# Seventeen groups of work in place of sixteen, the first and the last with one batch each

## The reference

```
x = x + layernorm(attn(layernorm(x)))
x = x + layernorm(ffn(layernorm(x)))

attn(x): x = x + lif(time_mix(layer_norm(x, ln1_s, ln1_b)))
         x = x + lif(channel_mix(layer_norm(x, ln2_s, ln2_b)))
  time_mix:    k, v, r = mixes of x and x shifted by one step, times Wk, Wv, Wr
               sigmoid(r) * wkv(w_decay, u_first, k, v) @ Wo     (a scan over time)
  channel_mix: sigmoid(xr @ Wr) * (square(relu(xk @ fWk)) @ fWv)     (128 -> 512 -> 128)
  lif:         a leaky integrate-and-fire scan over time that gives spikes 0 or 1
ffn(x):  h = silu(x @ w1) * (x @ w2)      (128 -> 512, ternary weights, a scale per output)
         h = gelu(h @ h1);  h = gelu(h @ h2)      (512 -> 512, twice)
         h @ w3                                   (512 -> 128)
```

## Time and profile before

| | |
|---|---|
| median of 3 runs | 652.96 us (652.8 to 653.86) |
| the profiled execution | 655.56 us, of which 653.6 us span from first to last instruction |
| PE busy | 585.9 us (90%), 2241 matmuls |
| DVE busy | 556.2 us (85%) |
| ACT busy | 535.6 us (82%) |
| POOL busy | 418.9 us (64%) |
| mean granted TensorE clock | 0.97 |
| HBM | 12.14 MB read, 4.19 MB written |

### The profile page before, as it was taken

The page is one execution under the profiler, slowest core; times in us unless marked ns, Lnnn a source line. Parts: engine busy times, 40 slices in busy tenths (PEclk is TensorE's granted clock), DMA queues, the critical chain, the costliest instruction groups (busy, mean ns, idle before and its releaser), DMA issues. The chain is left out here.

```text
span 653.6 us, 9756 instructions
## 1 busy us (share of the span) xinstructions
PE 585.9 (90%) x2241; PEld 361.9 (55%) x2241; DVE 556.2 (85%) x1538; ACT 535.6 (82%) x849; POOL 418.9 (64%) x571
## 2 busy tenths in 40 slices
PE   1366699999999999999999999999999999999994
PEld 0122256575656666565756565665756566656662
DVE  2978899989899999999999999999899899875543
ACT  4776587979798998979797988979797988967773
POOL 4553447677767768767677677686757675553442
PEclk9778799999999999999999999999999999999998
DMA  8010000000010101010000101010000101000001
GB/s 292 2 33 17 19 17 17 16 19 16 18 33 18 33 18 33 18 34 1 21 29 18 32 19 32 18 33 18 18 17 1 34 2 33 2 16 2 16 2 32
DMA packets 26574, 17.02 MB, mean 26 GB/s; under 512 B 1168, under 2 KB 25744, under 8 KB 26256
## 3 DMA queue, kind: packets, MB, share of 16 engines
q1 hardware_dynamic: 26512, 16.34, 8.1%
HBM read 12.14 MB, written 4.19 MB: 25 GB/s over the span
## 5 line engine op out<-in xcount | busy, mean ns | idle before, releaser
L906 ACT ACTIVATE hid<-p_f,scale 128x512 f32<-128x512 f32 x128 | 87.9, 687 | 65.0 <-PE p_f L2255 64.6
L2255 PE MATMUL p_f<-a_lo,w_hi 128*128 128x512 f32 x320 | 134.2, 419 | 1.6 <-DVE a_lo L289 0.7
L2255 PE MATMUL p_f<-a_hi,w_hi 128*128 128x512 f32 x320 | 125.9, 394 | 0.0
L2255 PE MATMUL p_f<-b_lo,w_hi 128*128 128x512 f32 x256 | 111.4, 435 | 2.3 <-DVE b_lo L289 0.9
L2255 PE MATMUL p_f<-b_hi,w_hi 128*128 128x512 f32 x256 | 100.6, 393 | 0.0
L900 ACT ACTIVATE a_hi<-hid 128x512 fp32r<-128x512 f32 x128 | 79.1, 627 | 2.9 <-DVE hid L1640 1.6
L432 POOL TENSOR_TENSOR nd<-factors,pq 128x512 f32<-128x512 f32 x32 | 38.7, 1210 | 63.3 <-DVE pq L1507 63.3
L289 DVE TENSOR_TENSOR a_lo<-hid,a_hi 128x512 fp32r<-128x512 f32 x96 | 65.6, 703 | 9.5 <-ACT a_hi L900 8.9
L2255 PEld LDWEIGHTS p_f<-a_lo,w_hi 128*128 128x128 f32 x320 | 60.3, 188 | 21.1 <-issue 7.0
L416 POOL TENSOR_TENSOR rstd<-var,minus_half 128x4 f32<-128x4 f32 x64 | 70.0, 1098 | 2.2
L289 POOL TENSOR_TENSOR b_lo<-hid,b_hi 128x512 fp32r<-128x512 f32 x32 | 45.4, 1430 | 38.7 <-DVE fired_all L1548 26.3
(11 more groups left out here) (143 smaller groups left out, 1437.5 us busy)
## 6 DMA issues: line engine op xcount, KB each, us to landing
xa<-in_x SPq DMA_DIRECT2D x16, 256.0 KB, 2.8
xb<-in_x SPq DMA_DIRECT2D x16, 256.0 KB, 3.1
out<-y_out SPq DMA_DIRECT2D x15, 256.0 KB, 3.5
kk<-in_ffn SPq DMA_DIRECT2D x1, 1024.0 KB, 7.0
hid<-in_ffn SPq DMA_DIRECT2D x1, 1024.0 KB, 9.6
mix<-in_mix SPq DMA_DIRECT2D x1, 512.0 KB, 6.2
gate<-in_ffn SPq DMA_DIRECT2D x1, 512.0 KB, 5.6
mix<-in_mix SPq DMA_DIRECT2D x1, 320.0 KB, 3.8
```

The lines of the kernel that those rows point to most:

```text
L906: act.activation(hid[:, m], p_f[m % 2][:, :], ACT.Gelu, scale=scale[:, 1 + layer, m:m + 1]).then_inc(s_gelu[layer], 1)
L2255: last = pe.matmul(out_, w[:, b], x[:, k], start=(k == 0 and t == 0), stop=(k == n - 1 and t == len(terms) - 1))
```

## The change

There are 17 groups. Group 0 and group 16 hold one batch (256 columns, two token tiles); groups 1 to 15 hold two. Every instruction of a one-batch group is cut to `0:g.w` columns, `0:g.nb` batches or `0:g.j` tiles; its number of instructions stays, except that what is issued per tile or per batch is issued half as often. The written orders of all engines are laid anew, in `opening`, `onset`, `turn` and `ending`; turn still runs for i = 5 to 12, and the ending has one more group. In the last group the two blocks of each hidden layer that are computed first are taken in parts (three input blocks each, then the fourth). Its last product takes the fourth input block as one fp32 product from `hid` itself, so its `high(3, 3)` and `low(3, 3)` are gone. Its statistics are taken from `p_turn` directly, and the copy to tokens runs after them.

Cut to its core:

```diff
-GROUPS_IN_ALL = 16
+GROUPS_IN_ALL = 17
+ROWS = 256
+TILES = 2
...
         self.par = n % 2
         self.turn = n // 2
+        self.nb = 1 if n in (0, GROUPS_IN_ALL - 1) else 2
+        self.first = max(2 * n - 1, 0)
+        self.w = self.nb * ROWS
+        self.j = self.nb * TILES
...
-    GROUPS = B // NB
+    GROUPS = B // NB + 1
...
-    x_tiles = x_in.rearrange("(g b) (h p) c -> g p (b h) c", b=NB, p=P)
-    out_tiles = out.rearrange("(g b) (h p) c -> g p (b h) c", b=NB, p=P)
+    def tiles(t, g):
+        return t[g.first:g.first + g.nb].rearrange("b (h p) c -> p (b h) c", p=P)
...
-                sp.dma_start(xa[:, g.par], x_tiles[g.n]).then_inc(s_xa[g.par], 16)
+                sp.dma_start(xa[:, g.par, 0:g.j], tiles(x_in, g)).then_inc(s_xa[g.par], 16)
...
-                sp.dma_start(out_tiles[GROUPS - 1][:, 2 * h:2 * h + 2],
-                             y_out[:, 2 * h:2 * h + 2]).then_inc(s_stored, 16)
+                sp.dma_start(tiles(out, G[GROUPS - 1])[:, h:h + 1], y_out[:, h:h + 1]).then_inc(s_stored, 16)
             sp.wait_ge(s_stored, 16 * (GROUPS + 1))
...
-                act.activation(hid[:, m], p_f[m % 2][:, :], ACT.Gelu,
+                act.activation(hid[:, m, 0:g.w], p_f[m % 2][:, 0:g.w], ACT.Gelu,
                                scale=scale[:, 1 + layer, m:m + 1]).then_inc(s_gelu[layer], 1)
...
+            def last_tokens(g):
+                act.wait_ge(s_bn[5], g.n + 1)
+                wait(act, s_y_out, g.n)
+                act.activation(f_out[:, 0:g.j], p_turn[:, 0:g.w].rearrange("p (j c) -> p j c", c=C),
+                               ACT.Copy).then_inc(s_f_out, 1)
...
+            def last_stats(g):
+                dve.wait_ge(s_turned[5], g.n + 1)
+                statistics(5, g, bn5, p_turn[:, 0:g.w].rearrange("p (j c) -> p j c", c=C))
...
             def last_norm(g, h):
 
+                dve.wait_ge(s_f_out, g.n + 1)
                 dve.wait_ge(s_shift5, g.n + 1)
                 dve.wait_ge(s_rstd[5], g.n + 1)
-                for j in (2 * h, 2 * h + 1):
+                for j in (h,):
                     last = dve.tensor_scalar(f_out[:, j], f_out[:, j], rstd5[:, j:j + 1], shift5[:, j:j + 1], ALU.mult,
                                              ALU.add)
                 last.then_inc(s_last_n, 1)
@@ -1664,8 +1765,7 @@
 
                 dve.wait_ge(s_last_n, h + 1)
                 wait(dve, s_stored, 16 * g.n)
-                dve.tensor_tensor(y_out[:, 2 * h:2 * h + 2], f_out[:, 2 * h:2 * h + 2],
-                                  xres[:, g.par, 2 * h:2 * h + 2], ALU.add).then_inc(s_last_out, 1)
+                dve.tensor_tensor(y_out[:, h:h + 1], f_out[:, h:h + 1], xres[:, g.par, h:h + 1], ALU.add).then_inc(s_last_out, 1)
 
...
+                def hidden_part(layer, g, m, blocks):
+
+                    hi, lo = (b_hi, b_lo) if layer == 2 else (a_hi, a_lo)
+                    first = (H1 if layer == 1 else H2) + m * HB
+                    for k in blocks:
+                        if m == 0:
+                            pe.wait_ge(s_hi[layer], HB * g.n + k + 1)
+                            pe.wait_ge(s_lo[layer][k], g.n + 1)
+                        terms = [(w_hi, lo), (w_hi, hi)] + ([(w_lo, lo), (w_lo, hi)] if general else [])
+                        for t, (w, x) in enumerate(terms):
+                            last = pe.matmul(p_f[m][:, 0:g.w], w[:, first + k], x[:, k, 0:g.w], start=(k == 0 and t == 0),
+                                             stop=(k == HB - 1 and t == len(terms) - 1))
+                    if HB - 1 in blocks:
+                        last.then_inc(s_h[layer], 1)
 
                 def last_product(g):
 
-                    split_product(p_f[0][:, :], range(W3, W3 + HB), a_hi, a_lo, 3, g).then_inc(s_w3, 1)
+                    split_product(p_f[0], range(W3, W3 + HB), a_hi, a_lo, g, 3).then_inc(s_w3, 1)
+
+                def last_product_end(g):
+
+                    for k in range(HB - 1):
+                        pe.wait_ge(s_hi[3], HB * g.n + k + 1)
+                        pe.wait_ge(s_lo[3][k], g.n + 1)
+                        terms = [(w_hi, a_lo), (w_hi, a_hi)] + ([(w_lo, a_lo), (w_lo, a_hi)] if general else [])
+                        for t, (w, x) in enumerate(terms):
+                            pe.matmul(p_f[0][:, 0:g.w], w[:, W3 + k], x[:, k, 0:g.w], start=(k == 0 and t == 0), stop=False)
+                    k = HB - 1
+                    pe.wait_ge(s_gelu[2], HB * (g.n + 1))
+                    weights = [w_hi] + ([w_lo] if general else [])
+                    for t, w in enumerate(weights):
+                        last = pe.matmul(p_f[0][:, 0:g.w], w[:, W3 + k].bitcast(F32), hid[:, k, 0:g.w], start=False,
+                                         stop=(t == len(weights) - 1))
+                    last.then_inc(s_w3, 1)
 
```

The repeated turn, PE:

```diff
                 def turn(g):
 
+                    after(pe, s_gelu[2], g[4].n, HB, 3)
+                    last_product(g[4])
                     after(pe, s_relu[1], g[2].n)
                     channel_k(g[2], 3)
-                    after(pe, s_gate, g[4].n, HB, 4)
-                    v_product(g[1])
+                    after(pe, s_f_cm, g[4].n)
+                    to_gate(g[3], 0)
                     after(pe, s_f0_hi, g[3].n)
                     after(pe, s_f0_lo, g[3].n)
                     turn_5(g[4])
-                    after(pe, s_f_cm, g[4].n)
-                    to_gate(g[3], 0)
+                    after(pe, s_relu[2], g[2].n)
+                    channel_v(g[2], 0)
+                    channel_v(g[2], 1)
                     after(pe, s_gelu[2], g[4].n, HB, 4)
                     to_value(g[3], 0)
                     after(pe, s_bv[0], g[1].n)
+                    after(pe, s_bv[1], g[1].n)
                     to_gate(g[3], 1)
-                    after(pe, s_relu[2], g[2].n)
-                    channel_v(g[2], 0)
-                    channel_v(g[2], 1)
                     after(pe, s_relu[3], g[2].n)
                     to_value(g[3], 1)
+                    channel_v(g[2], 2)
                     after(pe, s_gate, g[3].n, HB, 1)
                     to_gate(g[3], 2)
                     after(pe, s_swiglu, g[3].n, HB, 1)
                     to_value(g[3], 2)
                     after(pe, s_gate, g[3].n, HB, 2)
                     to_gate(g[3], 3)
-                    channel_v(g[2], 2)
                     after(pe, s_swiglu, g[3].n, HB, 2)
                     to_value(g[3], 3)
                     channel_v(g[2], 3)
@@ -2576,68 +2759,70 @@
                     r_product(g[1])
                     after(pe, s_tanh_r, g[0].n)
                     channel_k(g[1], 0)
+                    after(pe, s_gate, g[3].n, HB, 4)
+                    v_product(g[0])
                     after(pe, s_tanh_r2, g[1].n)
                     channel_k(g[1], 1)
                     after(pe, s_relu[0], g[1].n)
                     channel_k(g[1], 2)
                     after(pe, s_z2, g[1].n)
                     turn_4(g[2])
-                    after(pe, s_gelu[2], g[3].n, HB, 3)
-                    last_product(g[3])
 
```

The opening, DVE, at its start and before the first group's `f0`:

```diff
             def opening():
 
@@ -1674,211 +1774,210 @@
                 mix_1(G[0], 0)
                 mix_1(G[0], 1)
                 mix_1(G[0], 2)
+                low_weights(0)
+                maximum(G[0])
                 stats_1(G[1])
                 moments_1(G[1])
-                maximum(G[0])
                 excess(G[0])
                 bounds(G[0])
-                low_weights(0)
+                low_weights(1)
+                terms(G[0], 0)
+                terms(G[0], 1)
+                sum_over_time(G[0], 1)
                 scaled_weights(0)
-                low_weights(1)
-                sum_over_time(G[0], 1)
-                terms(G[0], 1)
-                terms(G[0], 0)
                 sum_over_time(G[0], 0)
+                stats_1(G[2])
                 denominator(G[0])
-                stats_1(G[2])
                 numerator(G[0])
                 ratio(G[0])
                 ratio_end(G[0])
-                low_weights(2)
+                moments_1(G[2])
                 fire(0, G[0])
+                fired_flag(0, G[0])
                 mix_1(G[1], 0)
-                fired_flag(0, G[0])
-                moments_1(G[2])
...
                 stats_3(G[0])
+                moments_3(G[0])
                 add_1(G[1])
-                moments_3(G[0])
                 stats_2(G[1])
                 moments_2(G[1])
                 maximum(G[2])
                 mix_1(G[2], 1)
                 norm_2(G[1])
-                residual_3(G[0])
                 mix_1(G[2], 2)
+                stats_1(G[4])
                 excess(G[2])
                 mix_2(G[1], 0)
                 mix_2(G[1], 1)
+                residual_3(G[0])
                 stats_4(G[0])
+                bounds(G[2])
                 moments_4(G[0])
                 relu(G[1], 0)
-                bounds(G[2])
+                rest_flag()
```

(102 more changed lines are left out.)

1285 lines of the change are left out of this document (708 added, 577 removed).

## The result

The changed kernel is slower. Its median is 659.47 us (657.81 to 660.37, four runs), beside 653.17 us (652.8 to 653.86) for the kernel before on the same chip: ratio 1.0087, 95% interval 1.0072 to 1.0103. The forecast was 646.8 us with a range up to 655.0; it missed on the other side. The profiled execution took 660.37 us with a span of 658.8; against the 653.6 of before that is 5.2 us more, where the sum said 6.2 less.

The account below looks back on a forecast made before the run. PE was taken to bound the kernel, DVE 2.5 us behind, with room only at both ends; -17.5 + 16.7 - 3.9 + 0.5 - 2.0 = -6.2 us took the median from 652.96 to 646.8 us, range 640.5 to 655.

Parts of the forecast that it names:

- Step 1: Opening: paced by DVE; with group 0 halved, group 1's first gate product comes 17.5 us earlier, at 101.5 us.
- Rival C: Opening doesn't profit: DVE's idle time stays at 24.7 us, low clock lasts; 652.7 us, no change; chance 0.12.
- Step 2: PE behind group 1's gate: group 0 34.6 before, 18.3 after; `channel_v` 2.85; work 2.2 larger; 16.7 us later.
- the factor: Period over PE's priced work for a group, 1.045, used to scale the rest of PE's work.
- Step 5: Turn: v product between `channel_k` 0 and 1, DVE's terms ahead of the last scan; -2.0 us in eight turns.
- Step 4: Rest of the ending: keeps 8 us over PE's priced work, adds 0.5 us for one stretch more.
- Step 3: Last stretch, from gate to end: from 34.4 to 20.6 us; over the factor -3.9 us.
- Rival A: Turn: gate waits 0.6 us until `output_scaled` empties `p_f0`, 7.2 us in 12 periods; 656.0 us; chance 0.17.
- Rival B: Narrow matmuls: weight loads pace them at 0.189 us; +4.5 us, 651.3 us; chance 0.11.

Follow-up runs that it names:

- v_early: Kernel before with only the turn's v product moved between the first two `channel_k` for groups 5 to 12: 655.03 us, ratio 1.0017.
- after_again: The changed kernel itself, unaltered, timed once more beside the kernel before: 658.17 us, ratio 1.0061.
- low_first: Changed kernel with POOL's low half of block 1 of group 11's first hidden layer ahead of group 10's offset and norm: 657.28 us, ratio 1.0043.
- combined: Changed kernel with old turn order, POOL's low half and group 12's neurons earlier, last hidden layers whole, last two lows swapped: 654.63 us, ratio 1.0000.
- plain_tail: Changed kernel with last group's layers whole, last block split into high and low, statistics from copied tokens: 658.79 us, ratio 1.0065.
- after: The changed kernel itself, as first measured against the kernel before: 659.47 us, ratio 1.0087.
- old_turn: `low_first` with the eight turns of every engine in the order of the kernel before: 655.22 us, ratio 1.0015.
- combined3: `combined` with the v product moved between the first two `channel_k` in the old turn's order, groups 5 to 12: 654.73 us, ratio 1.0019.

## Why the prediction was wrong

The bound was read right: PE, with DVE close behind, and both ends with room. What failed is the assumption that a newly laid order keeps the old one's excess. By the prediction's steps:

- **Step 1, right, with some luck in the size.** Group 1's first gate product came at 102.18 us, forecast 101.5, 16.9 earlier than before. Up to there DVE is busy 79.8 us against 94.3, 14.5 less (forecast 14.1), and idle 22.4 against 24.7 (2.3 less, forecast 3.4). Other executions are less kind: over the ten traces with this opening the point lies between 101.7 and 104.1 us, and in `v_early`, which has the opening of before, at 117.14 and not 119.05. From 16 us to group 0's first gate product the clock was 0.87 here and 0.71 in `after_again`, and the stretch took 54.3 and 54.0 us: there the low clock costs nothing, as it should be if DVE paces the opening. Rival C is out in its time; that DVE's idle time hardly falls it had half right.
- **Step 2, right in size at the ends, not in between.** Its own terms (34.6, 18.3, 2.85, 2.2) give 15.7 more and not 16.0, which changes the forecast by 0.4 us. The priced work is 2.2 us more, as said, and each stretch more brings its own 1.5 of excess. The stretch from group 1 to 2 exceeds it by 3.0 where the factor gave 1.4.
- **Step 5 failed in its mechanism.** That the v product's move "takes up some of the 0.49 us of waits" rested on PE's wait for `bv` and on the bound 0 for the other end. The move alone makes the period 0.11 longer (`v_early`). In the changed kernel the new order exchanged `bv` for `n`, more of `mixed`, and once `b_lo` and `f_cm`: 6.8 us of waits in eight periods against 3.9. The eight stretches' excess is 14.7, forecast 10.4, before 11.7. The bounds (0 to 0.49) excluded a loss without a reason; that was the fault, 4.3 us.
- **Step 4 failed.** "I keep the 8 and add 0.5" took the new ending for the old one. It has 19.1 us of excess, forecast 17.0. In it the stall of group 11 has 3.7 more than in `low_first`, 2.9 of them low clock that not every execution has; without that the new ending is better than I priced it.
- **Step 3, half right.** 34.4 to 23.0 us, forecast 20.6. The gates took 4.1 (4.5). From there to the last product's last wait it took 10.5 (8.0): ACT's alternation of gelu and high, 0.9 a block, the parts, and DVE's order. The tail took 8.3 (8.1).
- **Rival A** (the gate waits for `f_cm`) was the right kind with the wrong place and price. In the changed kernel it waits once, 0.4 us; in `v_early` it is `turn_5` that waits, 0.16 a period.
- **Rival B is out.** The narrow matmuls of the last group start 0.118 us apart (ten steps from 640.10 to 641.28), forecast 0.122, though each has a weight load of about 0.19:

```profile
640.34 0.28 PE L2438 MATMUL p_f<-a_hi,w_hi 128*128 128x256 f32 x1
640.45 0.28 PE L2438 MATMUL p_f<-a_lo,w_hi 128*128 128x256 f32 x1
640.57 0.28 PE L2438 MATMUL p_f<-a_hi,w_hi 128*128 128x256 f32 x1
```

```profile
L2438 PEld LDWEIGHTS p_f<-a_hi,w_hi x8: 187/188/192, 638.7 to 641.2; 128*128 128x128 f32 x8
```

By the Trainium skill ("TensorE: Matmul & The Clock Gate", "What overlaps and what doesn't"), which has loads overlap matmuls only where the row group differs, they would be 214 ns apart, by the prediction's estimate; the trace disagrees here as it did at 512 columns.

The five terms 0.6 + 1.6 + 4.3 + 2.1 + 2.4 make 11.0 of the 11.4 us by which the span (658.8) missed the one of the sum (653.6 - 6.2); the rest is rounding.

What stays open: `combined` still has 1.7 us more excess to the gate of group 1 than forecast, 1.7 in the stretch behind it, and 2.5 in the turns and their joins. Why the kernel before itself moves (medians 653.17, 655.15, 654.39 and 653.3 us, single runs from 652.5 to 656.1) was not looked into; the 1.9 us between its opening and that of `v_early` are of that size. Ratios of 0.1 to 0.2% are at the edge of what these runs tell. What decides whether the clock falls is open too.

## What to carry to other kernels

A hand-laid order has an excess of its own, some us in 500, and it is not inherited: after re-laying, price each stretch again and list the new waits, and forecast the old excess only where the order is the old one. A wait that a profile puts down to a late operand says nothing of the step that feeds that operand unless the operand's own engine waited for it: look there first. Where DVE and POOL both work on tensors in SBUF, look at which started first. When work is halved at the ends, orders and widths have to change together, so test a re-laid part at its own width.

## What the runs showed of the chip that was not expected

- The clock may or may not fall behind the same stall: PE busy 1.6 of 4 us with waits of 1.64 and 0.99 us, and then 0.53 granted for 7 us in the first trace and alike in `plain_tail`, 1.00 in two others. One execution can't tell whether such a stall costs 0.8 us or 3.7.
- The opening shows the same. From group 0's to group 1's first gate product identical opening orders took 31.6 to 31.9 us (`after`, `plain_tail`, `old_turn`, `combined3`; clock 0.95 in the changed kernel) or 33.0 to 33.3 (`after_again`, `low_first`, `combined`, and others; 0.91).
- DVE and POOL slow each other: the same two low halves took 3.28 us with POOL's sum and shift beside them and 1.49 without, and POOL's sum took 1.71 us beside them and 1.30 in `low_first`. The Trainium skill ("SBUF — State Buffer", "SBUF: two separate sides") has the two share a port pair as an exclusive lock, where a DVE operation with two SBUF inputs meets a POOL operation that reads SBUF: who starts first has it for the whole operation. A low half has two such inputs, and the trace agrees: taken singly, DVE's two end at 478.38 and 480.07 us, each 0.55 to 0.56 behind the end of a POOL operation (477.82 and 479.52). With POOL ahead by 0.18 us at 371.85, PE had to wait 1.0 us at 376.71. A step moved on POOL can lengthen one on DVE without any semaphore between them.
